# Attention in trips of 64 queries and four batches, with plain float32 scores, ahead of a recurrence

## The chip, the cores and the metric

The kernel runs on one core of one Trainium2 chip. Times are device microseconds of that core, from one launch. The core has five engines that run their own instruction streams: PE (TensorE, matrix products; PEld are its weight loads), DVE (VectorE), ACT (ScalarE), POOL (GpSimd) and SP (SyncE, which here only issues DMAs). They wait for one another by semaphores.

## The reference

Eight batches of 512 tokens with 512 features pass a causal attention layer with 16 heads of 32 features, and then a recurrence over the 512 tokens. Each result is added to its input. cond is one vector for each batch; it gives the attention one key and one value more ("image"), and the recurrence its first state.

```python
q_word, k_word, v_word = jnp.split(x @ c_attn_w + c_attn_b, 3, axis=-1)
k = jnp.concatenate([k_img, k_word], axis=1)       # k_img, v_img: from cond
v = jnp.concatenate([v_img, v_word], axis=1)
scores = jnp.einsum('bhqd,bhkd->bhqk', q, k) / jnp.sqrt(jnp.float32(HDIM))
scores = jnp.where(causal[None, None], scores, jnp.float32(MASK_OUT)) + mask
attn = jax.nn.softmax(scores, axis=-1)
out = jnp.einsum('bhqk,bhkd->bhqd', attn, v)
out = out.transpose(0, 2, 1, 3).reshape(B, S, EMBED)
x = x + (out @ c_proj_w + c_proj_b)

xw = jnp.einsum('ntd,dh->nth', x, Wx) + b
def step(prev_h, xw_t):
    next_h = jnp.tanh(prev_h @ Wh + xw_t)
    return (next_h, next_h)
x = x + hs                                           # hs: all 512 states, from h0 = cond
```

## The kernel before

**Tiling.** Attention runs in 16 trips. A trip takes 128 queries (one block of tokens) of two batches, blocks outermost, so that four trips finish a block for all eight batches. In a trip stand 32 units, one for each batch and head. Causality lets a unit of block p (0 to 3) look at 128 (p + 1) keys. A unit is a score product (`score`, L928), a subtraction with mask and row minimum on DVE (L791), the exponential with its sum on ACT (L648), transposes of 128 columns each (`turn`, L938) whose copies alternate between DVE (L800) and ACT (L655), and, for each group of four units, value products (`pv`, L951): for every key tile four products, one for each head, with 32 weight columns each, so in four column groups of the array.

**Precision.** Projections run as three products of float32r halves (`split_product`, L466 to L468). For the scores, q and k are split too: ACT writes the high halves (L641), DVE the low ones (L766), and six DMAs for each chunk of four heads store them in `kq_dram` (L478). Three DMAs bring a group's tile back (L540), with the three parts under one another in 96 partitions, and one float32r product of 96 rows makes a unit's scores. The scores of the image key are four short products for each chunk (L915, L917). Value products, recurrence and input products are plain float32 products.

**Recurrence.** A step (L1004) is 16 plain products with 32 weight columns, four for each of the four column groups of the array, from the states to `rec`; DVE transposes the result (L842), ACT takes the tanh (L694), and the next step needs that. Every four steps share input products (`xsteps`, L995, 16 products; `xpart` is a quarter of them). Tokens of block b can be stepped when block b is through attention, so its 128 steps are spread over the four trips of block b + 1 (STEPS = 32 a trip). The steps from FIRST = 384 on stand after the last trip, alone.

**Order.** `main_order` lays the events of a trip out by unit: transposes lag four units behind the scores, value products ten; at unit 10 the projection of the trip before begins (`proj`, L835 on DVE), behind it the load of x for the next but one trip (`xload`, L520), at unit SPLIT_AT the next trip's x is split (`xsplit`, L628 on ACT), and from unit 10 + FREE the next trip's q, k and v are made. `order` spreads the steps evenly over the estimated cost and turns this into one list for each engine; each engine works through its list in order. LAGS shifts an engine's list against PE's. SP issues the loads of key and value tiles as places come free: tile groups in a ring of ROOM columns (`tile_places`), values in VTILES buffers.

## Time and profile before

| | us |
|---|---|
| median of 3 runs | 1697.04 |
| lowest, highest | 1691.76, 1697.95 |
| the profiled execution | 1689.44 |
| its span, first to last instruction | 1687.6 |

The profile has one execution. Its rows give, for each instruction or group of instructions, the line of the kernel, the engine, what is written and read, and the count; PE's busy time includes the latency at the end of a product, so two blocks that follow one another closely overlap in it, and a block's own time is better read as the distance to the next start. A plain float32 product stands as two instructions in the records (the 16 products of a step are x32), a float32r product or a transpose as one. "Idle before" names what ended an engine's wait.

### The profile page before, as it was taken

The page shows a single profiled execution, that of the slowest core. Times are in us where ns is not written, and L with a number is a line of the kernel's source. Part 1 is how long each engine was busy: PE and PEld are TensorE (multiplying, and loading weights), DVE is VectorE, ACT ScalarE, POOL GpSimd, SP SyncE. Part 2 cuts the span into 40 slices and gives each one's busy share as a digit, 9 for nine tenths or more (in the row PEclk, how much of TensorE's full clock was granted, in tenths as well). Part 3 has the DMA queues.
Part 4 walks back from the last instruction along what each step waited for, and adds up shares of the span by engine and source line. Part 5 has one row for each costly group of instructions (what it writes and reads, how often), then busy time and mean ns, then how long its engine had stood idle before and what let it go on. Part 6 is the DMA issues. An engine that isn't in the chain of part 4 may idle for free.

```text
span 1687.6 us, 65682 instructions
## 1 busy us (share of the span) xinstructions
PE 1521.2 (90%) x28397; PEld 1288.2 (76%) x28397; DVE 817.9 (48%) x2592; ACT 718.4 (43%) x2289; POOL 369.9 (22%) x535
## 2 busy tenths in 40 slices
PE   6589988999999999999999988999999999777775
PEld 6478777778877878888888877888888788666664
DVE  4455554454545455555555545555565555222221
ACT  3355553444444444544445444454454545111111
POOL 2045552203131222203132130311313100000000
PEclk9799899999999999999999999999999999999999
DMA  7655555334344454445545445555555632000000
GB/s 252 184 186 179 166 181 145 111 96 124 106 126 116 120 145 132 129 110 144 143 137 151 112 136 148 142 156 133 151 140 156 165 89 70 9 15 10 15 9 15
DMA packets 139936, 204.73 MB, mean 121 GB/s; under 512 B 19432, under 2 KB 91240, under 8 KB 139136
## 3 DMA queue, kind: packets, MB, share of 16 engines
q1 hardware_dynamic: 112640, 128.05, 28.9%
q0 software_dynamic: 27008, 72.47, 13.0%
q8 instruction: 226, 3.70, 1.0%
q14 instruction: 62, 0.51, 0.1%
HBM read 133.06 MB, written 67.37 MB: 119 GB/s over the span
## 4 chain that ended last, share of the span: by engine, by line
PE 79%; DMA 6%; DVE 5%; issue 4%; ACT 4%; SPq 2%; POOL 0%; DVEq 0%; ACTq 0%; POOLq 0%
PE rec L1004 24%; PE turned L938 10%; PE dense L466 7%; PE dense L467 6%; PE dense L468 6%; PE rec L995 5%; PE scores L928 5%; PE pv L951 4%; PE scores L1004 4%; DMA xin<-x 3%; DVE pre L842 3%; ACT states L694 2%; PE pv L969 2%; DMA kq<-kq_dram 1%; PE dense L1011 1%
## 5 line engine op out<-in xcount | busy, mean ns | idle before, releaser
L1004 PE MATMUL rec<-wh,states 128*32 128x128 f32 x14336 | 485.2, 276 | 62.9 <-ACT states L694 61.3
L1004 PEld LDWEIGHTS rec<-wh,states 128*32 128x32 f32 x14336 | 376.0, 110 | 129.1 <-ACT states L694 90.7
L648 ACT ACTIVATE probs<-probs,nmax 128x128 f32<-128x128 f32 (+3 forms) x512 | 287.4, 562 | 209.5 <-DVE nmax L791 203.0
L694 ACT ACTIVATE states<-pre 128x32 f32<-128x32 f32 x512 | 133.3, 260 | 431.3 <-DVE pre L842 430.3
L842 DVE STREAM_TRANSPOSE pre<-rec 128x128 f32<-128x128 f32 x448 | 141.6, 316 | 342.1 <-PE rec L1004 338.9
L791 DVE CUSTOM_DVE_ANT_0 probs<-scores,msk,nimg 128x128 f32<-128x128 f32 (+3 forms) x512 | 276.2, 544 | 61.8 <-PE scores L928 54.5
L938 PE MATMUL turned<-ident,probs 128*128 128x128 f32 x1280 | 243.7, 290 | 13.1 <-ACT probsT L655 11.7
L928 PE MATMUL scores<-kq 96*128 96x128 f32 (+3 forms) x512 | 204.9, 403 | 18.5 <-DMA kq<-kq_dram 16.7
L938 PEld LDWEIGHTS turned<-ident,probs 128*128 128x128 f32 x1280 | 145.4, 141 | 78.8 <-issue 55.7
L800 DVE COPY probsT<-turned 128x128 f32<-128x128 f32 (+3 forms) x256 | 124.6, 487 | 80.1 <-PE turned L938 75.7
L655 ACT COPY probsT<-turned 128x128 f32<-128x128 f32 (+3 forms) x256 | 107.0, 418 | 95.8 <-PE turned L938 94.2
L995 PE MATMUL rec<-wx,x 128*32 128x128 f32 x3584 | 131.7, 278 | 10.9 <-ACT rec L620 10.7
L466 PE MATMUL dense<-xT_hi,wqkv_hi 128*128 128x256 f32 x464 | 139.8, 301 | 0.6 <-DVE ks_lo L766 0.6
L478 POOL DMA_DIRECT2D kq_dram<-qs_hi x120 | 86.3, 722 | 224.2 <-DVE qs_lo L766 215.1
L467 PE MATMUL dense<-xT_lo,wqkv_hi 128*128 128x256 f32 x464 | 135.1, 291 | 0.0
L468 PE MATMUL dense<-xT_hi,wqkv_lo 128*128 128x256 f32 x464 | 134.3, 290 | 0.0
L928 PEld LDWEIGHTS scores<-kq 96*128 96x128 f32 x512 | 103.0, 201 | 36.9 <-DMA kq<-kq_dram 17.9
L591 POOL DMA_DIRECT2D out<-outs x32 | 20.4, 639 | 490.4 <-ACT outs L684 490.4
L995 PEld LDWEIGHTS rec<-wx,x 128*32 128x32 f32 x3584 | 101.9, 134 | 27.2 <-issue 13.5
L478 POOL DMA_DIRECT2D kq_dram<-ks_hi x120 | 86.5, 721 | 87.9 <-DVE ks_lo L766 87.5
L951 PE MATMUL pv<-probsT,vbuf 128*32 128x128 f32 x2560 | 98.0, 281 | 7.8 <-DMA vbuf<-v_dram 7.8
L648 ACT ACTIVATION_READ_ACCUMULATOR probs<-probs,nmax 128x1 f32 x512 | 95.9, 187 | 0.0
(159 smaller groups left out, 2218.6 us busy)
## 6 DMA issues: line engine op xcount, KB each, us to landing
kq<-kq_dram SPq DMA_DIRECT2D x96, 320.0 KB, 5.2
kq<-kq_dram SPq DMA_DIRECT2D x96, 256.0 KB, 4.4
kq<-kq_dram SPq DMA_DIRECT2D x96, 192.0 KB, 3.6
kq_dram<-qs_hi POOLq DMA_DIRECT2D x120, 128.0 KB, 2.9
kq_dram<-ks_hi POOLq DMA_DIRECT2D x120, 128.0 KB, 3.4
kq<-kq_dram SPq DMA_DIRECT2D x96, 128.0 KB, 2.8
xin<-x SPq DMA_DIRECT2D x32, 256.0 KB, 4.0
v_dram<-vbuf POOLq DMA_DIRECT2D x32, 256.0 KB, 3.1
```

Source lines behind the costliest of these rows:

```text
L466: pe.matmul(out, hi, moving_hi, start=first, stop=False)
L467: pe.matmul(out, hi, moving_lo, start=False, stop=False)
L468: return pe.matmul(out, lo, moving_hi, start=False, stop=last)
L478: eng.dma_start(kq_dram[part, r, :, i, :, at:at + P], src[:, i % 2, :].bitcast(F32).rearrange("p (e t) -> p e t", e=2)).then_inc(stored[i ...
L648: act.activation(probs[:, g % PROBS, 0:n], probs[:, g % PROBS, 0:n], ACT.Exp, scale=-1.0, bias=nmax[:, e, h:h + 1], accum_out=rowsum[:, e, ...
L694: act.activation(state_cells(g), pre[:].rearrange("p f (b z) -> p f b z", z=GROUP)[:, :, :, s], ACT.Tanh).then_inc(h_ready, 1)
L791: dve.tensor_tensor_reduce(out=probs[:, g % PROBS, 0:n], in0=scores[g % 2][:, 0:n], in1=msk[:, e, 0:n], scale=-SCALE, scalar=nimg[:, trip ...
L842: dve.transpose(pre_all, rec_bank(g // GROUP)[:, 0:P]).then_inc(pre_ready, 1)
L928: pe.matmul(scores[g % 2][:, 0:n], heads_tile(group)[0:3 * Q, j, 0:P], heads_tile(group)[0:3 * Q, j, P:P + n], start=True, stop=True).then ...
L938: last = pe.transpose(turned[g % 2][:, P * k:P * k + P], probs[:, g % PROBS, P * k:P * k + P], ident[:])
L995: pe.matmul(rec_bank(g)[Q * j:Q * j + Q, 0:P], x1_group(g)[:, f], wx[:, f, :].rearrange("p (a j c) -> p a j c", a=C, j=C)[:, :, j, :], sta ...
L1004: last = pe.matmul(rec_bank(g // GROUP)[Q * j:Q * j + Q, 0:P], state_tile(g - 1)[:, f, :], wh[:, f, P * j:P * j + P], start=False, stop=f ...
```

## The change

A trip takes 64 queries of four batches. There are still 16 trips and 32 units in each; a unit is now one head of two batches, whose 64 queries each fill the 128 partitions. Blocks become parts of 64 tokens, so key lengths run from 64 to 512 in steps of 64, and the transposes and value products of an odd number of parts end with half a tile. The steps of a part are spread over the two trips of the next part, 32 in each, and FIRST is 448: 64 steps stand after the last trip.

q stays in SBUF in float32 (ACT adds the bias), k is written once by DVE, stored by one DMA for each chunk and loaded by one DMA for each group; the splits, `kq_dram` and their semaphores go. Scores are plain float32 products: for each unit two, one for each batch, with the 32 rows of the head (a row group of the array) and 64 weight columns (half of the column groups). Units are emitted in pairs, whose heads lie in neighbouring row groups. Image scores are four plain products for each chunk. Value products are for one batch and 64 queries, so twice as many with half the columns. x is loaded in four pieces for each trip, since a trip takes half of the tokens of two of the stored tiles. VTILES is 2, with two batches in each buffer; the ring of key tiles holds three of the longest.

```diff
-TRIPS = BLOCKS * PAIRS
+W = P // 2
+PARTS = S // W
+QUADS = 2
+PAIRED = 2
+TRIPS = PARTS * QUADS
...
-STEPS = S // (BLOCKS * PAIRS)
+STEPS = W // QUADS
...
-FIRST = (BLOCKS - 1) * P
-
-PROBS = 4
+FIRST = S - W
+
+PROBS = 5
...
-FREE = (7, 5, 5, 5, 5)
-SPLIT_AT = (15, 14, 14, 14, 14)
-VTILES = 3
+SPLIT_AT = (16, 16, 15, 15, 15, 15, 15, 15)
+CHUNK_AT = (18, 18, 16, 16, 16, 16, 16, 16)
+VTILES = 2
...
         if u < HEADS:
+            if u % 2 == 0:
+
+                emit([("score", v, 0, 0.07 + 0.107 * keys(g) / P) for v in (u, u + 1)])
             if u % HC == HC - 1:
                 loads += [("kqload", group, 0, 0.0) for group in range(GROUPS) if PLACES[group][0] == u // HC + 1]
-            emit([("score", u, 0, max(0.11, 0.053 * (block_of(g) + 1)) + 0.1)])
...
-        def store_parts(eng, kind, g, i):
...
+        def store_keys(eng, g, i, stored):
+            p, r = divmod(g, QUADS)
+            eng.dma_start(k_dram[4 * r:4 * r + 4, i, :, W * p:W * p + W].rearrange("b p t -> p b t"),
+                          knew[:, i, :].rearrange("p (b t) -> p b t", b=4)).then_inc(stored, 16)
...
+        def load_x(eng, g):
+
+            p, r = divmod(g, QUADS)
+            for k in range(2):
+                for pair in range(PAIRED):
+                    eng.dma_start(xin[:, g % 2, pair, 2 * k:2 * k + 2, :].rearrange("p f (e t) -> p (f e) t", e=2),
+                                  x[p // 2 * PAIRS + 2 * r + pair, :, 2 * k:2 * k + 2, :]
+                                  .rearrange("p f (e t) -> p (f e) t", e=2)[:, :, W * (p % 2):W * (p % 2) + W]
+                                  ).then_inc(x_loaded[g % 2][k], 16)
...
-                    for part in range(3):
-                        sp.dma_start(heads_tile(g)[Q * part:Q * part + Q].bitcast(F32),
-                                     kq_dram[part, r, :, c, e, 0:P + P * (p + 1)]
-                                     .rearrange("(j d) t -> d j t", d=Q)).then_inc(tile_loaded[g % LOADS], 16)
+                    sp.dma_start(heads_tile(g), k_dram[4 * r + 2 * e:4 * r + 2 * e + 2, c, :, 0:keys(trip)]
+                                 .rearrange("b p t -> p b t")).then_inc(tile_loaded[g % LOADS], 16)
...
+                    whole, left = divmod(keys(trip), P)
+                    for b in range(2):
+                        mine = v_dram[4 * r + 2 * e + b, 0:keys(trip), P * c:P * c + P]
+                        if whole:
+                            sp.dma_start(vtile[g % VTILES][:, b, 0:whole, :],
+                                         mine[0:P * whole].rearrange("(n q) d -> q n d", q=P)
+                                         ).then_inc(v_loaded[g % VTILES], 16)
+                        if left:
+                            sp.dma_start(vtile[g % VTILES][0:left, b, whole, :], mine[P * whole:P * whole + left]
+                                         ).then_inc(v_loaded[g % VTILES], 16)
...
-                elif kind in ("q", "k"):
+                elif kind == "q":
                     wait_dense(act, kind, g, i)
...
+                    act.activation(q[:, g % 2, i, :], bank(kind, g, i)[:, 0:2 * P], ACT.Identity,
+                                   bias=bqk[:, 0, i:i + 1]).then_inc(copied(kind, g, i), 1)
...
+                elif kind == "k":
+                    wait_dense(dve, kind, g, i)
+                    if g:
+                        wait_stored(dve, g - 1, i)
+                    dve.tensor_scalar(knew[:, i, :], bank(kind, g, i)[:, 0:2 * P], bqk[:, 1, i:i + 1], None,
+                                      ALU.add).then_inc(copied(kind, g, i), 1)
...
+                        for b in range(2):
+
+                            n = 2 * e + b
+                            last = pe.matmul(d[W * b:W * b + W, HC * e:HC * e + HC], q[:, g % 2, i, W * n:W * n + W],
+                                             kimg[:, i, 4 * r + n, :], start=True, stop=True, skip_group_check=True)
...
-                    pe.matmul(scores[g % 2][:, 0:n], heads_tile(group)[0:3 * Q, j, 0:P],
-                              heads_tile(group)[0:3 * Q, j, P:P + n], start=True, stop=True).then_inc(scores_ready, 1)
+
+                    rows = slice(Q * j, Q * j + Q)
+                    for b in range(2):
+                        at = W * (2 * e + b)
+                        last = pe.matmul(scores[g % 2][W * b:W * b + W, 0:n], q[rows, trip % 2, c, at:at + W],
+                                         heads_tile(group)[rows, b, :], start=True, stop=True, skip_group_check=True)
+                    last.then_inc(scores_ready, 1)
...
+                    for at in range(0, n, P):
+                        last = pe.transpose(turned[g % 2][0:min(P, n - at), at:at + P],
+                                            probs[:, g % PROBS, at:min(at + P, n)], ident[:])
...
+                    for at in range(0, n, P):
+                        rows = slice(0, min(P, n - at))
+                        for b in range(2):
+                            mine = slice(at + W * b, at + W * b + W)
+                            for j in range(HC):
+
+                                last = pe.matmul(pv[Q * j:Q * j + Q, P * c + W * b:P * c + W * b + W],
+                                                 vtile[g % VTILES][rows, b, at // P, Q * j:Q * j + Q],
+                                                 probsT[rows, (HC * g + j) % TURNED, mine],
+                                                 start=c == 0 and b == 0 and at == 0, stop=False, skip_group_check=True)
```

PE's stream, in a trip with 384 keys before (between a step and the next projection products). Transposes write turned, scores go to scores0 and scores1, L1004 is the step.

```order
L1004 MATMUL rec<-wh,states 32x128 x16
L938 MATMUL turned1<-ident,probs 128x128 x3
L928 MATMUL scores1<-kq 128x384
L951 MATMUL pv<-probsT,vbuf 32x128 x12
L1004 MATMUL rec<-wh,states 32x128 x16
L1011 MATMUL dense0<-ident,hist 128x128 x4
L938 MATMUL turned0<-ident,probs 128x128 x3
L928 MATMUL scores0<-kq 128x384
...
L938 MATMUL turned1<-ident,probs 128x128 x3
L928 MATMUL scores1<-kq 128x384
L938 MATMUL turned0<-ident,probs 128x128 x3
L928 MATMUL scores0<-kq 128x384
```

The same place in a trip with 320 keys of the change; L963 are the scores, L974 the transposes, L991 the value products, L1035 and L1044 input products and step.

```order
L1044 MATMUL rec<-wh,states 32x128 x16
L991 MATMUL pv<-probsT,vbuf 32x64 x24
L974 MATMUL turned0<-ident,probs 128x128 x2
L974 MATMUL turned0<-ident,probs 64x128
L963 MATMUL scores0<-kt,q 64x320 x2
L1035 MATMUL rec<-wx,x1 32x128 x16
L1044 MATMUL rec<-wh,states 32x128 x16
L963 MATMUL scores1<-kt,q 64x320 x2
...
L963 MATMUL scores0<-kt,q 64x320 x2
L1044 MATMUL rec<-wh,states 32x128 x16
L1051 MATMUL dense0<-ident,hist 128x128 x4
L963 MATMUL scores1<-kt,q 64x320 x2
```

One 96x128-weight score for each unit has become two of 32x64, shown as x2; a pair stands together or has a step or other products between its units.

SP's list at the start, before: six stores and three loads stand ahead of the first scores.

```order
L511 DMA x1<-w_proj 128x512 [waits low_ready]
L511 DMA x1<-w_proj 128x512 x3
L478 DMA kq_dram<-qs_hi 128x2x128 [waits dense_copied0]
L478 DMA kq_dram<-qs_hi 128x2x128
L478 DMA kq_dram<-qs_lo 128x2x128
L478 DMA kq_dram<-ks_hi 128x2x128 [waits dense_copied1]
L478 DMA kq_dram<-ks_lo 128x2x128
L478 DMA kq_dram<-ks_hi 128x2x128
L540 DMA kq<-kq_dram 32x4x256 [waits k_stored_first0,q_stored_first0]
L540 DMA kq<-kq_dram 32x4x256 x2
```

SP's list at the start, with the change:

```order
L542 DMA x1<-w_proj 128x512 x4
L498 DMA k_dram<-knew 128x4x64 [waits dense_copied1]
L568 DMA kt<-k_dram 128x2x64 [waits k_stored_first0] x2
L498 DMA k_dram<-knew 128x4x64 [waits dense_copied1]
L568 DMA kt<-k_dram 128x2x64 [waits k_stored_first1]
L498 DMA k_dram<-knew 128x4x64 [waits dense_copied1]
L568 DMA kt<-k_dram 128x2x64 [waits k_stored_first2]
```

Ahead of the first tile stands one store, and a load is one DMA.

ACT's list ahead of the split of the next trip's x (`xT_hi`), before, in a trip with 256 keys:

```order
L694 ACTIVATE states<-pre 128x32 [waits hist_kept,pre_ready]
L648 ACTIVATE probs,rowsum<-probs,nmax 128x256 [waits shifted_ready]
L694 ACTIVATE states<-pre 128x32 [waits pre_ready]
L648 ACTIVATE probs,rowsum<-probs,nmax 128x256 [waits shifted_ready]
L694 ACTIVATE states<-pre 128x32 [waits pre_ready]
L684 COPY outs<-dense1 128x4x4x32 [waits out_stored,dense_ready]
L620 COPY rec<-kimg 128x128 [waits pre_ready]
L694 ACTIVATE states<-pre 128x32
L655 COPY probsT<-turned1 128x256 [waits pv_done,turned_ready]
L628 CAST xT_hi<-xin 128x512 [waits dense_ready,x_loaded0_0]
L628 CAST xT_hi<-xin 128x512 [waits dense_ready,x_loaded0_1]
```

ACT's list at the same place with the change, in a trip with 192 keys:

```order
L724 ACTIVATE states<-pre 128x32 [waits hist_kept,pre_ready]
L724 ACTIVATE states<-pre 128x32 [waits pre_ready]
L676 ACTIVATE probs,rowsum<-probs,nmax 128x192 [waits shifted_ready] x2
L724 ACTIVATE states<-pre 128x32 [waits pre_ready]
L714 COPY outs<-dense1 128x4x4x32 [waits out_stored,dense_ready]
L659 COPY rec<-bxrows 128x128 [waits pre_ready]
L724 ACTIVATE states<-pre 128x32
L683 COPY probsT<-turned1 128x256 [waits pv_done,turned_ready]
L724 ACTIVATE states<-pre 128x32 [waits hist_kept,pre_ready]
L666 CAST xT_hi<-xin 128x512 [waits dense_ready,x_loaded0_0]
L666 CAST xT_hi<-xin 128x512 [waits dense_ready,x_loaded0_1]
```

The split (two instructions, the last rows) stands one unit later in the change, behind one step more; the probabilities of the next units are queued behind it in both.

## Rows read from the trace of the kernel before

**Rows 1.** The page's first part: busy time and share of the span.
```profile
PE 1521.2 (90%) x28397; PEld 1288.2 (76%) x28397; DVE 817.9 (48%) x2592; ACT 718.4 (43%) x2289; POOL 369.9 (22%) x535
```
**Rows 2.** Stretches: us, busy PE, PEld, DVE, ACT, POOL, PEclk, DMA share, GB/s.
```profile
75.00:267.00 192.00, 175.63 (x1379) 149.79 (x1378) 107.63 (x480) 103.73 (x402) 86.74 (x128) 0.92 0.56 174
267.00:1460.00 1193.00, 1141.81 (x21966) 966.73 (x21966) 630.51 (x1880) 549.84 (x1673) 266.73 (x376) 0.99 0.46 126
1460.00:1687.00 227.00, 159.32 (x4800) 132.51 (x4800) 50.32 (x151) 40.88 (x158) 4.78 (x8) 0.99 0.05 12
```
**Rows 3.** Chain of waits in a bare step: start us, us, what; last row: PE's timeline.
```profile
1500.15 1.13 PE rec L1004 x32
...
1501.30 0.33 DVE pre L842
...
1501.65 0.27 ACT states L694
...
1501.96 1.12 PE rec L1004 x32
...
1501.05 0.40 PE L995 MATMUL scores<-wx,x 128*32 128x128 f32 x8
```
**Rows 4.** PE's timeline (start us, busy us, line, tiles, count), untiled float32 products.
```profile
29.68 3.68 PE L906 MATMUL turned<-wh,spread 128*128 128x512 f32 x8
```
**Rows 5.** PE's timeline in the window of 1500.14 to 1500.18 us.
```profile
1500.15 0.32 PE L1004 MATMUL rec<-wh,states 128*32 128x128 f32 x4 [0.51 <-ACT states L694]
```
**Rows 6.** PE's timeline across changes of tiling, from 901 us.
```profile
901.32 0.49 PE L938 MATMUL turned<-ident,probs 128*128 128x128 f32 x3
901.73 1.08 PE L1004 MATMUL rec<-wh,states 128*32 128x128 f32 x32
902.75 0.44 PE L928 MATMUL scores<-kq 96*128 96x384 f32 x1
...
903.91 0.55 PE L938 MATMUL turned<-ident,probs 128*128 128x128 f32 x3
```
**Rows 7.** PE's timeline: input products and the step behind them.
```profile
910.17 1.14 PE L995 MATMUL rec<-wx,x 128*32 128x128 f32 x32
911.12 1.06 PE L1004 MATMUL rec<-wh,states 128*32 128x128 f32 x32
```
**Rows 8.** PE's timeline around scores of 384 and of 128 columns.
```profile
1005.81 0.55 PE L938 MATMUL turned<-ident,probs 128*128 128x128 f32 x3
...
1006.37 0.17 PE L915 MATMUL dense<-kimgx,qs_hi 128*128 128x8 f32 x1
...
1006.74 0.55 PE L938 MATMUL turned<-ident,probs 128*128 128x128 f32 x3
...
91.56 0.33 PE L938 MATMUL turned<-ident,probs 128*128 128x128 f32 x1
...
91.79 0.33 PE L466 MATMUL rec<-xT_hi,wqkv_hi 128*128 128x256 f32 x1
```
**Rows 9.** PE's timeline around a score of 512 columns (it lies between).
```profile
1290.33 0.66 PE L938 MATMUL turned<-ident,probs 128*128 128x128 f32 x4
...
1291.14 1.08 PE L1004 MATMUL rec<-wh,states 128*32 128x128 f32 x32
```
**Rows 10.** Groups by line and form: value products, all of them.
```profile
L951 PE MATMUL pv<-probsT,vbuf 128*32 128x128 f32 x2560 | 98.0, 281 | 7.8 <-DMA vbuf<-v_dram 7.8
```
**Rows 11.** Waits of ACT: us in total, times, longest.
```profile
ACT xT_hi L628 <- DMA xin<-x: 37.3, 18, 3.3
```
**Rows 12.** Timeline of SP and of PE around the second split of x.
```profile
120.64 0.83 SPq L520 DMA_DIRECT2D xin<-x  x2
...
125.63 0.30 PE L938 MATMUL turned<-ident,probs 128*128 128x128 f32 x1 [3.88 <-ACT probsT L655]
```
**Rows 13.** PE's timeline: the first scores and the first value products.
```profile
47.88 0.47 PE L928 MATMUL scores<-kq 96*128 96x128 f32 x1 [8.01 <-DMA kq<-kq_dram]
...
71.62 0.66 PE L951 MATMUL pv<-probsT,vbuf 128*32 128x128 f32 x8 [7.76 <-DMA vbuf<-v_dram]
```

More of the change, by code:

```diff
@@ L75, in tile_places @@
     for group in range(GROUPS):
[L76 removed]
+        size = 2 * keys(group // 8)
         if at + size > ROOM:
@@ L86, with v_loads @@
 PLACES = tile_places()
+def v_loads():
+    counts = []
+    for group in range(GROUPS):
+        n = keys(group // 8)
+        mine = 2 * (n // P > 0) + 2 * (n % P > 0)
+        counts.append(mine + (counts[group - VTILES] if group >= VTILES else 0))
+    return counts
+V_LOADS = v_loads()
 def main_order():
@@ L176, in order @@
     place = {}
-    for b in range(BLOCKS - 1):
-        first = ends[(b + 1) * PAIRS - 1] + 1
-        for n in range(PAIRS):
-            last = begins[(b + 1) * PAIRS + n]
+    for b in range(PARTS - 1):
+        first = ends[(b + 1) * QUADS - 1] + 1
+        for n in range(QUADS):
+            last = begins[(b + 1) * QUADS + n]
             whole = sum(w for *_, w in main[first:last])
@@ L198, in put @@
         for name, lags in LAGS.items():
-            if kind in ("q", "k") and name == ("POOL" if g == 0 else "SP"):
+            if kind == "k" and name == ("POOL" if g == 0 else "SP"):
                 continue
@@ L318, in attention_recurrence @@
         vnew = vbuf[:, 0:2 * D].rearrange("p (e d) -> p e d", e=2)
-        vtile = [vbuf[:, 2 * D + n * BLOCKS * P:2 * D + (n + 1) * BLOCKS * P].rearrange("p (n d) -> p n d", d=P)
-                 for n in range(VTILES)]
+        vtile = [vbuf[:, 2 * D + 2 * n * BLOCKS * P:2 * D + 2 * (n + 1) * BLOCKS * P]
+                 .rearrange("p (b n d) -> p b n d", b=2, d=P) for n in range(VTILES)]
         rinvx = spread[:, 0, :].rearrange("p (h q) -> p h q", h=H)
@@ L501, in _ @@
                 if n == C:
-                    for k in range(2):
-                        sp.dma_start(xin[:, 0, 2 * k:2 * k + 2, :], x[0, :, 2 * k:2 * k + 2, :]
-                                     ).then_inc(x_loaded[0][k], 16)
+                    load_x(sp, 0)
                 f, half = divmod(i, 2)
@@ L936, in _ @@
                         pe.wait_ge(turned_copied[g % 2], g // 2)
[L937 to L938 removed]
+                    for at in range(0, n, P):
+                        last = pe.transpose(turned[g % 2][0:min(P, n - at), at:at + P],
+                                            probs[:, g % PROBS, at:min(at + P, n)], ident[:])
                     last.then_inc(turned_ready, 1)
                 elif kind == "pv":
[L941 removed]
+                    n = keys(g // 8)
                     c = g % C
```

299 lines of the change are left out of this document (129 added, 170 removed).

## The prediction

> **What bounds the kernel now.** I read the page's busy shares first [rows 1]: TensorE is busy for 90% of the span, VectorE for 48%, ScalarE for 43%. Cut into stretches [rows 2], the span has three regimes. Up to 75 us the kernel starts up. From 75 to 267 us run the trips without recurrence steps, with TensorE busy for 176 of 192 us. From 267 to 1460 us attention and 384 recurrence steps share TensorE, which is busy for 1142 of 1193 us. The last 227 us are 128 steps with nothing beside them, and there one step follows the other through three engines: the chain [rows 3] shows 1.13 us of products, 0.33 of VectorE's transpose, 0.27 of ScalarE's tanh, and the next step starts 1.81 us after the one before. So a step costs 1.81 us when it stands alone, and only its time on TensorE when it is hidden. Up to 1460 us the question is how much TensorE has to do; the other engines wait for it. Busy counts the latency at the end of each block, so I price TensorE's work by distances between starts.
>
> **Two facts about TensorE that carry the sum.** First, the price of a plain float32 product. It is recorded as two instructions (16 products of a step are x32). Eight such records, 512 columns wide and untiled, take 3.68 us [rows 4], so about 0.43 us each, 0.84 ns a column. A step's 32 records of 128 columns take 0.90 us until the next block starts [rows 3]; alone at 0.84 ns a column they would take 3.4. Thus four column groups run at once and a record costs 0.027 us. A window of 0.04 us at a step's start holds the starts of four records [rows 5].
> Second, changing the tiling costs time. Transposes take some 0.109 us each (four are busy 0.66, three 0.55 [rows 6, 9]), yet the step behind three of them starts 0.41 us after the first, 0.08 more than 0.33 [rows 6]. The 32 records of that step hand over to an untiled score after 1.02 us, where a handover within the tiling took 0.90 [rows 3, 6], so 0.12 more. Three transposes behind another tiling are busy 0.55 us, behind the same one 0.49 [rows 6], 0.06 more; and a step behind another tiling 1.08 against 1.06 [rows 6, 7]. In and out is 0.28 us, 0.14 for each change. This speaks against the change. The Trainium skill says the same ("TensorEngine Tiling (Array Packing)", Key Properties: changing the tiling mode drains TensorE) without a price; by the rows the trace agrees.
>
> **The change part by part,** against the profiled span of 1687.6 us (its run took 1689.4; the median of the runs shown is 1697.0).
> (a) 64 of the 128 exposed steps go: 64 x 1.81 = -116. They come back in the hidden part at 0.90 each, +58, with their 16 groups of input products, which were spread over idle time and now stand as blocks of 32 records: 0.95 us from such a block to the step [rows 7], 16 x 0.90 = +14 with the first load taken with the changes.
> (b) Tiling changes. In the built programs the rows x columns of neighbouring TensorE instructions change 887 times before and 1539 times after: every pair of scores is an island of 32x64 among transposes and steps, image scores become 128x64, and odd parts end a value product with 64 rows. 652 x 0.14 = +91. Nothing hides it. The tilings 32x64 and 64x32 stand nowhere in the trace; for a change to them I take the price of 128x32, and for its bounds 0.08 and 0.20 (the dearest in-step above together): +52 to +130.
> (c) Scores go away: a 384-column score between transposes and the next untiled block adds 0.23 us (0.56 less 0.33), a 128-column one 0.12 [rows 8], a 512-column one 0.28 (0.81 less 0.44 and the 0.09 of a change) [rows 9]; with 0.18 in between for 256, 128 x (0.12 + 0.18 + 0.23 + 0.28) = -104.
> (d) New scores: per unit two products (two batches, 64 columns of the array each), so four records of n columns at 0.84 ns. n is 64 to 512 and 288 in the mean, against 320 before. How many of the four tiles (two row groups, two column groups) run at once is the open point: no instruction of the trace uses row groups beside each other. From below, all eight records of a pair at once as fast as one, 0.84 n a pair: 61 us in all. From above, column halves together but row groups in turn: 512 x 1.67 x 288 = 246. I take what independent tiles give, as column groups do in [rows 3]: a pair costs two records' depth, 1.67 n, and a unit that stands alone the same. The new order has 199 pairs back to back and 114 units alone (a step or a block of x products between them): 313 x 1.67 x 300 = +157.
> (e) Image scores: four products limited by weight loads, 0.37 us [rows 8], 64 times, about -26; eight short records with half as many weight columns, two tiles at once, about +14. Net -12.
> (f) Value products double in number with 64 instead of 128 columns: 2560 records x 0.109/4 = 70 us before [rows 10], 5120 records after. If a record keeps to its columns, 0; if four cannot start faster than in 0.109 us, +70. Four started within 0.04 us [rows 5], so I take 0. The number of transposes stays 1280, as half tiles still stream 128 columns of the identity.
> The TensorE page of the Trainium skill ("TensorE: Matmul & The Clock Gate", Wait — 56ns, not 53.3ns?) has a floor of about 25 ns between starts, by which the value products would not gain from fewer columns. Four starts within 40 ns [rows 5] speak against it; a burst is no stream.
> (g) DVE and ScalarE: the q and k splits go (two of VectorE's operations for each column chunk, and one of ScalarE's two), key lengths fall by a tenth, the x1 writes come in four pieces instead of two, and VectorE stays near half busy. They lie beside TensorE: 0. What they can change is waits.
> (h) Waits. TensorE was idle for 98 of the first 1460 us (75 to 1460: 67.6 us by [rows 2]; the rest in the start). ScalarE waits 37.3 us for x in 18 places, as its queue is in order and probabilities stand behind [rows 11]; TensorE follows with gaps such as 3.88 us at 125.6 [rows 12]. x is asked for at 120.64, when the projection of two trips ago is copied, and split two units later. The split now comes one to two units later, so with 3 us a unit most of this is gone although the x load is in four DMAs of 256-byte pieces. About -34. The first scores waited 8.01 us for their tile behind six stores and three loads, the first values 7.76 us [rows 13]; now one store and one load go before it: about -12. SP queues behind its waits for value products, as before.
> Sum: -116 + 58 + 14 + 91 - 104 + 157 - 12 + 0 - 55 = **+33 us**: 1721 for the span, and 1697 + 33 = 1730 beside the median.
>
> **The rivals.**
> R1, row groups or halves overlap more than I take. Four records of one unit started together in [rows 5]; if these belong to two tiles only, a unit needs 0.84 n and standing alone costs nothing: 512 x 0.84 x 288 = 123, 34 less, 1696, no change. For: the burst. Against: a record would then run at twice the untiled rate. R1b, the other side: eight records of a pair at once, 61 us, 96 less, 1634. It decides from about 113 us for all scores.
> R2, row groups take turns: 246, +89, 1819. For: nothing in the trace shows them together. The Trainium skill ("TensorE: Matmul & The Clock Gate", Measured speedup vs the span model) has 3.07x for four row groups, against R2; no row here shows it.
> R3, the value products don't get shorter, (f): +67 to +70, 1800. That is what the floor above would give; the sum of it is made of [rows 5, 7].
> R4, the waits stay: the x load with its small pieces and the shared dense banks keep ScalarE waiting, +55, 1785. Or they vanish: -43, 1687.
> That the change doesn't do what it says: the 64 steps can't all fit. Seven parts of 64 steps in 14 trips of over 80 us is 32 x 1.81 = 58 us of chain a trip; they fit.
>
> **How the numbers follow.** Forecast 0.38, R1 0.22, R1b 0.11, R2 0.13, R3 0.07, R4 0.06 and 0.03. The error of (b) and (h) is about 30 us on each. Measurement of this kernel can tell about 0.5% (8.5 us) from no change. Faster by over 0.5%: R1b, a third of R1, a seventh of the forecast and half of what is left, 0.29. Within: 0.14. Slower: 0.57. The range leaves out half of R1b and half of R2 and the ends: 1645 to 1815. The likeliest case alone has 1700 to 1762.
>
> **What would show it.** The last stretch of bare steps should be 64 x 1.81 = 116 us. The scores' blocks in the timeline: start to next start near 1.67 n ns for a pair (0.8 us at n = 512 plus 0.14) and as much for a lone unit; half of it is R1, double R2. A value block of one key tile and eight products should last 0.22 us to the next start; 0.44 is R3. ScalarE's wait for x should be under 10 us and the first score start before 45 us; else R4. I am wrong as a whole if a change of tiling around the scores costs far less than 0.14.

## The result, and the profile after

The changed kernel takes 1743.5 us (median of 4 runs, 1733.6 to 1749.6), the kernel before 1695.6 beside it: a ratio of 1.028, 95% interval 1.023 to 1.033. It is slower, by 48 us, where I had forecast 33. The profiled execution has a span of 1741.3 us, 53.7 more than before, and it is the one to take apart. First its page, part 1 (as [rows 1]), then the start and the three stretches of [rows 2], cut where the steps begin and where the last work beside them ends (us, busy PE, PEld, DVE, ACT, POOL, PEclk, DMA share, GB/s).

```profile
PE 1654.6 (95%) x32749; PEld 1263.7 (73%) x32749; DVE 798.4 (46%) x2687; ACT 670.5 (39%) x2257; POOL 184.6 (11%) x300
```
```profile
0.00:50.00 50.00, 35.70 (x249) 31.28 (x250) 19.14 (x49) 15.85 (x32) 11.47 (x26) 0.86 0.65 217
50.00:177.00 127.00, 115.89 (x1182) 90.73 (x1180) 57.68 (x282) 51.06 (x223) 19.18 (x34) 0.77 0.25 65
177.00:1613.00 1436.00, 1416.86 (x28741) 1073.56 (x28739) 694.18 (x2273) 581.73 (x1921) 150.99 (x235) 1.00 0.28 76
1613.00:1741.00 128.00, 86.14 (x2581) 68.15 (x2580) 27.37 (x84) 21.86 (x83) 2.98 (x5) 0.96 0.05 13
```

Start and step-free trips together shrink from 267 to 177 us, the tail of bare steps from 227 to 128, but the shared stretch grows from 1193 to 1436: it now carries 448 steps and 14 trips. TensorE is busy there for 98.7% of the time, so nothing but its own work counts. The table sums that work over all records, each from its start to the next record's start, with the waits between taken out (us). The waits are listed below it; "all else" is smaller work and the few us ahead of the first record and behind the last.

| on TensorE | before | after |
|---|---|---|
| scores | 138 | 210 |
| transposes of probabilities | 138 | 191 |
| image scores | 29 | 22 |
| value products | 87 | 95 |
| split products (q, k, v, projection) | 401 | 419 |
| steps | 501 | 504 |
| input products of the steps | 138 | 125 |
| waits in the last stretch | 59 | 32 |
| other waits | 92 | 38 |
| all else | 105 | 106 |

Scores and transposes took 125 us more; the waits gave back 80. Two places of the timeline show the new blocks (start, us busy, line, tiles, count): a pair of scores at n = 448, then a lone unit at the same n (n is the number of keys, so of columns); the pair at 1192.17 and the lone unit at 1198.05 repeat them.

```profile
1178.06 0.98 PE L963 MATMUL scores<-kt,q 32*64 32x448 f32 x8
1178.97 1.08 PE L1044 MATMUL rec<-wh,states 128*32 128x128 f32 x32
1179.98 1.09 PE L974 MATMUL turned<-ident,probs 128*128 128x128 f32 x8
...
1208.36 0.97 PE L963 MATMUL scores<-kt,q 32*64 32x448 f32 x4
1209.25 1.08 PE L1044 MATMUL rec<-wh,states 128*32 128x128 f32 x32
1210.27 0.97 PE L963 MATMUL scores<-kt,q 32*64 32x448 f32 x4
1211.16 0.39 PE L492 MATMUL dense<-xT_hi,wqkv_hi 128*128 128x256 f32 x1
```

Eight records take 0.91 us to the next start, four take 0.89. Over the medians of all blocks at each n from 128 to 512, a pair costs 1.667 n + 164 ns and a lone unit 1.667 n + 151 ns: the second unit of a pair costs 14 ns. The step between goes on to the next tiling after 1.01 us, where [rows 3] has 0.90 within one.

### The profile page after: what moved, and what is told of

The parts are those of the page before. It is cut to its first block, busy times and chain, and to the rows that moved or that the text cites. A ratio compares the mean times of both kernels' runs of the same rounds, so it can differ in the third digit from the quotient of the medians.

```text
span 1741.3 us, 74131 instructions
## 1 busy us (share of the span) xinstructions
PE 1654.6 (95%) x32749; PEld 1263.7 (73%) x32749; DVE 798.4 (46%) x2687; ACT 670.5 (39%) x2257; POOL 184.6 (11%) x300
## 4 chain that ended last, share of the span: by engine, by line
PE 89%; issue 3%; DVE 2%; DMA 2%; ACT 2%; SPq 1%; POOL 0%; DVEq 0%; ACTq 0%; POOLq 0%
PE rec L1044 26%; PE scores L963 11%; PE turned L974 11%; PE dense L492 8%; PE dense L493 7%; PE dense L494 7%; PE rec L1035 6%; PE pv L991 5%; PE pv L1009 2%; PE scores L1044 2%; DVE pre L870 1%; ACT states L724 1%; PE dense L945 1%; PE dense L1051 1%; SPq L517 1%
## 5 line engine op out<-in xcount | busy, mean ns | idle before, releaser
L1044 PE MATMUL rec<-wh,states 128*32 128x128 f32 x15360 | 516.4, 275 | 27.0 <-ACT states L724 25.8
L1044 PEld LDWEIGHTS rec<-wh,states 128*32 128x32 f32 x15360 | 399.7, 110 | 123.3 <-ACT states L724 64.3
L676 ACT ACTIVATE probs<-probs,nmax 128x64 f32<-128x64 f32 (+7 forms) x512 | 271.6, 531 | 269.7 <-DVE nmax L815 266.6
L815 DVE CUSTOM_DVE_ANT_0 probs<-scores,msk,nimg 128x64 f32<-128x64 f32 (+7 forms) x512 | 249.9, 514 | 62.8 <-PE scores L963 54.4
L974 PE MATMUL turned<-ident,probs 128*128 128x128 f32 (+1 forms) x1280 | 242.9, 292 | 7.9 <-ACT probsT L683 7.2
L963 PE MATMUL scores<-kt,q 32*64 32x64 f32 (+7 forms) x2048 | 231.4, 431 | 0.3 <-DVE nmax L815 0.2
L974 PEld LDWEIGHTS turned<-ident,probs 128*128 128x128 f32 (+1 forms) x1280 | 132.5, 135 | 90.4 <-issue 66.3
L1035 PE MATMUL rec<-wx,x 128*32 128x128 f32 x3840 | 133.7, 275 | 4.3 <-ACT rec L659 4.0
L1035 PEld LDWEIGHTS rec<-wx,x 128*32 128x32 f32 x3840 | 99.0, 109 | 29.5 <-ACT rec L659 12.0
L492 PEld LDWEIGHTS dense<-xT_hi,wqkv_hi 128*128 128x128 f32 x488 | 94.2, 193 | 24.1 <-issue 23.0
L991 PE MATMUL pv<-probsT,vbuf 128*32 128x64 f32 (+1 forms) x5120 | 104.9, 223 | 4.5 <-DMA vbuf<-v_dram 4.5
L963 PEld LDWEIGHTS scores<-kt,q 32*64 32x64 f32 x2048 | 65.2, 133 | 57.8 <-issue 48.0
L991 PEld LDWEIGHTS pv<-probsT,vbuf 128*32 128x32 f32 (+1 forms) x5120 | 84.8, 110 | 22.5 <-issue 16.0
L498 POOL DMA_DIRECT2D k_dram<-knew x60 | 47.0, 783 | 504.7 <-DVE knew L791 483.7
```

The lines of the kernel that those rows point to most:

```text
L492: pe.matmul(out, hi, moving_hi, start=first, stop=False)
L676: act.activation(probs[:, g % PROBS, 0:n], probs[:, g % PROBS, 0:n], ACT.Exp, scale=-1.0, bias=nmax[:, e, h:h + 1], accum_out=rowsum[:, e, ...
L815: dve.tensor_tensor_reduce(out=probs[:, g % PROBS, 0:n], in0=scores[g % 2][:, 0:n], in1=msk[:, e, 0:n], scale=-SCALE, scalar=nimg[:, trip ...
L963: last = pe.matmul(scores[g % 2][W * b:W * b + W, 0:n], q[rows, trip % 2, c, at:at + W], heads_tile(group)[rows, b, :], start=True, stop=T ...
L974: last = pe.transpose(turned[g % 2][0:min(P, n - at), at:at + P], probs[:, g % PROBS, at:min(at + P, n)], ident[:])
L991: last = pe.matmul(pv[Q * j:Q * j + Q, P * c + W * b:P * c + W * b + W], vtile[g % VTILES][rows, b, at // P, Q * j:Q * j + Q], probsT[rows ...
```

## The experiments

All ratios are to the kernel before, run on the same chip; "the changed kernel" stands at 1743 us, 1.028.

**1. Are row groups beside each other what makes a pair fast?** Both units of a pair read the same 32 rows.

```diff
-                    rows = slice(Q * j, Q * j + Q)
+                    rows = slice(Q * (j // 2 * 2), Q * (j // 2 * 2) + Q)
```

> Only the rows of the array that the second unit of each pair uses are changed: it reads the same 32 rows of q and keys as the first (so the scores of half the heads are those of the neighbouring head, and the output is another one). The order and the 1539 tiling changes are those of the changed kernel. Theory (the pair is fast since its units sit in different row groups): the pair costs 3.33 n + 0.16 us in place of 1.67 n + 0.16, 199 x 1.67 ns x 300 = +100 us, about 1843. Rival, the overlap has nothing to do with row groups (records of one unit leave gaps that any record can fill): 1743, no change.

Measured: 1815 us, ratio 1.073 (1.069 to 1.077), so +72 beside the median of the changed kernel. The timeline has pairs at n = 384:

```profile
1103.24 1.51 PE L963 MATMUL scores<-kt,q 32*64 32x384 f32 x8
1104.68 0.39 PE L492 MATMUL dense<-attnT_hi,wproj_hi 128*128 128x256 f32 x1
...
1113.85 1.51 PE L963 MATMUL scores<-kt,q 32*64 32x384 f32 x8
1115.29 0.87 PE L974 MATMUL turned<-ident,probs 128*128 128x128 f32 x6
```

A pair takes 1.44 us, which is 3.33 n + 0.16; by the formula above it takes 0.80 in different rows. Two row groups do run at once, and R2 (row groups in turn) falls by a direct test. My +100 for the sum took 300 columns for the mean of the pairs; it is 269, which gives +89, and TensorE's time in scores did grow by 87 us (210 to 297). That the kernel lost only 72 is mostly the clock: the split products took 8 us less, at a granted clock of 0.89 between 50 and 177 us instead of 0.77.

**2. Units one by one, and pairs never parted.** First every unit alone, as the scores were issued before the change; then no step between the two units of a pair.

```diff
-            if u % 2 == 0:
-                emit([("score", v, 0, 0.07 + 0.107 * keys(g) / P) for v in (u, u + 1)])
+            emit([("score", u, 0, 0.07 + 0.107 * keys(g) / P)])
```

> The scores are issued unit by unit, as before the change, never as a pair: 512 lone units in place of 199 pairs and 114 lone ones; tiling changes rise from 1539 to 1894. Theory (row groups run beside each other, a lone unit leaves half of them empty): 199 more runs of 1.67 ns x 288 = +96 us, 355 changes x 0.13 = +46, together +142: about 1885 us. Rival, row groups take turns anyway: only the changes, +46, 1790. Rival, a change of tiling costs nothing on its own: +96, 1840. The start of a lone unit to the next start should stay at 1.67 n + 151 ns.

```diff
                 done += main[at][3]
+                if main[at][0] == "score" and main[at][1] % 2 == 0 and at + 1 < last:
+                    continue
```

> No recurrence step is put between the two units of a pair of scores any more: 256 pairs and no lone unit, where the changed kernel has 199 pairs and 114 lone units; the tiling changes on TensorE fall from 1539 to 1480. Theory (four tiles, two row groups by two column halves, run at once, and a change of tiling costs 0.12 to 0.14 us): 57 runs of scores fewer at 1.67 ns x 300 columns = -28 us, and 59 x 0.13 = -8, so about 1707 us where the changed kernel takes 1743. Rival, row groups bring nothing (a pair lasts as long as two lone units): only the -8, 1735. Rival, the steps that now come in twos behind a pair wait for their chain of 0.9 us: up to 57 x 0.5 = 28 us come back, and TensorE's idle time grows from 70 us to near 100.

Measured: 1879 us (ratio 1.109, 1.106 to 1.113), +135 where the theory had +142; and 1704 us (1.007, 1.005 to 1.009), -40 by the medians and -36 by the ratios, where it had -36. TensorE's waits did not grow (74 us after 70), so the rival with steps that wait falls. So 36 to 40 of the 48 us that the change lost are the 57 pairs that its own step placement cut in two. Between these two kernels lie 256 runs of scores, 256 x 1.67 x 288 ns = 123 us, and 414 tiling changes; the 52 us left are 0.126 for a change, if a block more costs nothing else.

**3. What does a change of tiling cost by itself?** Small products of 4 columns were put ahead of the transposes of every unit, once on 32 rows and 32 columns, once untiled.

```diff
+                    pe.matmul(turned[g % 2][0:Q, 0:4], ident[0:Q, 0:Q], ident[0:Q, 0:4], start=True, stop=True, skip_group_check=True)
```
```diff
+                    pe.matmul(turned[g % 2][0:P, 0:4], ident[:], ident[:, 0:4], start=True, stop=True, skip_group_check=True)
```

> Ahead of the transposes of every unit, in the bank that they overwrite, stands one more product of 4 columns on 32 rows and 32 columns of the array: 512 products, and the tiling changes rise from 1539 to 2161. Its twin (the next kernel) has the same products untiled and no more changes. Theory (0.14 us for a change): 622 x 0.14 = 87 us more than its twin; by the order kernel, whose TensorE work fell 31 us for 372 changes, 0.084 each: +52. Rival, changes only cost where a long product drains: under +20 over its twin.

> The twin: the 512 products of 4 columns untiled, in the same places, 1539 tiling changes as in the changed kernel. Theory: a short untiled product costs some 0.05 us beside transposes, 512 x 0.05 = +26 us, about 1769 (from 1758 to 1785).

Measured: 1827 us (1.081, 1.077 to 1.085) with the islands, 1854 (1.096, 1.093 to 1.100) without them: the one with fewer changes is slower. Both theories missed, because the two are no twins. The timeline of the untiled one:

```profile
1200.35 0.39 PE L973 MATMUL turned<-ident 128*128 128x4 f32 x2
1200.59 0.53 PE L975 MATMUL turned<-ident,probs 128*128 128x128 f32 x3
...
1204.95 0.28 PE L973 MATMUL turned<-ident 128*128 128x4 f32 x2
1205.10 0.53 PE L975 MATMUL turned<-ident,probs 128*128 128x128 f32 x3
```

Four columns untiled cost 0.15 us among untiled blocks and 0.24 behind a step: 111 us for 512, 0.22 each, against my 0.05. The price of a short product is not in its columns. So I made a pair with equal products: 432 of them in the tiling of the steps, once ahead of transposes (1823 changes), once ahead of hidden steps (1539).

```diff
+                    if g >= HEADS - 432:
+                        pe.matmul(turned[g % 2][0:Q, 0:4], ident[:, 0:Q], ident[:, 0:4], start=True, stop=True, skip_group_check=True)
```
```diff
+                    if g < 432:
+                        pe.matmul(rec[0:Q, 256:260], ident[:, 0:Q], ident[:, 0:4], start=True, stop=True, skip_group_check=True)
```

> Ahead of the transposes of 432 units stands one product of 4 columns in the tiling of the steps (128 rows by 32 columns of the array). Where the block ahead has another tiling, it is an island: 1823 tiling changes in place of 1539. Its twin (the next kernel) has the same 432 products ahead of hidden steps, whose tiling they share, and 1539 changes. The difference between the two is 284 changes and nothing else. At 0.14 us each 40 us, at 0.084 (what the order kernel saved on TensorE for 372 changes) 24, at 0.12 34. Rival, a change costs only where a long product has to drain, not beside a short one: under 10 us.

> The twin: 432 products of 4 columns directly ahead of hidden steps, in their tiling, 1539 changes as in the changed kernel. Two records at the 0.027 us of a step's record are 0.06 us: 432 x 0.06 = +24 us if nothing else moves, 1767; if a record behind another of the same column tile has to wait for its end (0.11 us), +50 to +80.

The second opens an accumulation anew in the bank in which the steps accumulate, so its recurrent states are other ones; its instructions are the same. Measured: 1785 us (1.054, 1.051 to 1.057) and 1764 us (1.042, 1.039 to 1.045). The difference of 20.8 us over 284 changes is 0.073 us each (0.05 to 0.10 by the scatter of the runs); by the sums of TensorE's work (1717 and 1689 us) it is 0.097. So a change is not free, as the rival had it. But these are no exact twins either. Ahead of a step the trace shows of the small product

```profile
1154.79 0.19 PE L1043 MATMUL rec<-ident 128*32 128x4 f32 x1
1154.80 0.31 PE L1046 MATMUL rec<-wh,states 128*32 128x128 f32 x3
```

that three records of the step start between its two; it cost 0.043 us (18.5 us of work for 432). Ahead of transposes, behind a block of its own tiling (the first three lines) and between two blocks of transposes (the others), the timeline is this:

```profile
1154.54 1.06 PE L1046 MATMUL rec<-wh,states 128*32 128x128 f32 x32
1155.41 0.20 PE L974 MATMUL turned<-ident 128*32 128x4 f32 x2
1155.55 0.55 PE L976 MATMUL turned<-ident,probs 128*128 128x128 f32 x3
...
1170.68 0.55 PE L976 MATMUL turned<-ident,probs 128*128 128x128 f32 x3
1171.16 0.23 PE L974 MATMUL turned<-ident 128*32 128x4 f32 x2
1171.31 0.66 PE L976 MATMUL turned<-ident,probs 128*128 128x128 f32 x4
```

In the first case the step and the product take 1.01 us together, as a step alone does in the changed kernel. Over all places between 180 and 1600 us at which TensorE did not wait, the medians against the same places of the changed kernel are: +0.018 us where the product adds no change (behind steps and whole value products), +0.155 where it adds one (behind scores, image scores and half value products), +0.25 where it adds two (between untiled blocks). That is 0.137 for one change and 0.115 each for the two. With the product at 0.018 instead of 0.043, the twins would give 0.11 by the times and 0.13 by the work. So my 0.14 was somewhat high, not double.

**4. Exposed steps.** 64 steps go back into the tail, all else stays.

```diff
-FIRST = S - W
+FIRST = S - 2 * W
-    for b in range(PARTS - 1):
+    for b in range(PARTS - 2):
```

> The steps of the last two parts stand exposed at the end, 128 as before the change, the rest is the changed kernel's. Theory: 64 x 1.81 = +116 us, their 64 hidden steps go at 0.90 each, -58, and 16 groups of input products at 0.90, -14, which then stand in the idle time of the bare steps; 69 tiling changes fewer at 0.12, -8, and 11 runs of scores fewer, -6: together +30, about 1773 us where the changed kernel takes 1743. Last stretch 128 x 1.81 = 232 us. Rival, a hidden step costs more than its 0.90 (waits for its chain or drives the trips apart): then less than +15, under 1758. Rival, it costs nothing since it fills idle time of TensorE: +116, 1859.

Measured: 1767 us (1.044, 1.041 to 1.047), +24 by the medians and +28 by the ratios. Hiding the 64 steps is worth 24 to 28 us here, close to the +30 expected. So the change's other parts cost some 74.

**5. An order that follows the tiling.** If changes cost, an order with fewer should beat both kernels. Transposes come in twos, projections stand beside them, and a small dynamic programme places the steps.

```diff
+        if u % 2 == 0 and TURN_LAG <= u < HEADS + TURN_LAG:
+            emit([("turn", v, 0, 0.05 + 0.11 * tiles_of(v // UNITS)) for v in (u - TURN_LAG, u - TURN_LAG + 1)])
...
+        spots.append((at, done[-1], (before[at] != "column") + (after[at] != "column") - (before[at] != after[at])))
...
+                c = table[-1][p][0] + GAP_COST * max(0.0, GAP - work) ** 2
```

> The same work in an order that follows the tiling: the transposes of two units are issued together ahead of a pair of scores, what has no place of its own (projections, image scores) stands beside them, and a step goes where the tiling changes anyway or beside value products, spaced by a small dynamic programme; never within a pair. 256 pairs, no lone units, 1108 tiling changes in place of 1539. Theory (a change costs 0.12 to 0.14 us and nothing hides it): -28 for the lone units and 431 x 0.13 = -56, together -84: about 1659 us, faster than the kernel before (1696). Rival, changes of tiling are free or hidden: 1715. Rival, steps less evenly spread wait for their chain: each 0.2 us of wait on 448 steps gives back 90 us, and then TensorE's idle time of 70 us doubles.

Measured: 1714 us (1.013, 1.010 to 1.015), not 1659. Beside the kernel with pairs TensorE's work fell by 31 us. The expectation has 1108 changes; the program that ran has 1165, by the count that gives 1539 and 1480 for the kernels before it. So 31 us are for 315 changes, 0.099 each. But its waits rose from 74 to 117 us: the third case of the expectation, in small.

> The order that follows the tiling again, with steps kept at least 1.0 us of other work apart where this costs one tiling change (the first such kernel let TensorE wait 42 us more than the kernel with pairs only), image scores directly ahead of a pair of scores, transposes of the outputs beside other transposes, and x split one unit earlier: 1196 tiling changes, 256 pairs. Theory (a change costs 0.084 us as in the first such kernel, the waits go back to some 80 us): 1704 - 284 x 0.084 = 1680, with 5 to 10 us of waits 1685 to 1690, the time of the kernel before. Rival, waits stay at 110 us: 1710.

Measured: 1717 us (1.015, 1.013 to 1.018), the rival. The work stayed at 1597 us and the waits at 117, but they had moved. PE's timeline, and ACT's wait for x there, then in the changed kernel ([rows 11] for before), then in the next experiment:

```profile
1160.18 1.82 PE L1104 MATMUL rec<-wh,states 128*32 128x128 f32 x32 [3.86 <-ACT states L784]
```
```profile
ACT xT_hi L726 <- DMA xin<-x: 41.2, 24, 5.6
```
```profile
ACT xT_hi L666 <- DMA xin<-x: 16.8, 18, 3.6
```
```profile
ACT xT_hi L726 <- DMA xin<-x: 6.1, 5, 2.1
```

My own edit had caused it: I had moved the split of x a unit earlier, to where x had not landed, and tanh stands behind it in ScalarE's queue.

```diff
-SPLIT_AT = (15, 15, 14, 14, 14, 14, 14, 14)
-CHUNK_AT = (18, 18, 16, 16, 16, 16, 16, 16)
+SPLIT_AT = (16, 16, 16, 16, 16, 16, 16, 16)
+CHUNK_AT = (18, 18, 18, 18, 18, 18, 18, 18)
```

> The second order kernel with one thing moved: x is split for the next trip at unit 16 and its first products start at unit 18, where e_order2 had 14 and 16. In e_order2 ScalarE's in-order queue stood at the split until x had landed, and once a trip a recurrence step waited 2 to 4 us behind it (12 gaps of 2.0 to 4.1 us, about 40 us in all). Theory: these gaps go, TensorE's idle time falls from 117 to about 80 us, the time from 1717 to about 1680, faster than the kernel before by 10 us. Rival, the first products of a trip now come too late for its first scores: gaps at the start of each trip instead, 1700 to 1720.

Measured: 1687 us, ratio 0.998 (0.996 to 1.000), the time of the kernel before; waits 98 us. Of the 31 us won, 20 are waits; TensorE's work fell too, at a mean granted clock of 0.987 after 0.979. What was left showed on ScalarE and TensorE around one step:

```profile
1036.40 0.61 ACT L736 ACTIVATE probs<-probs,nmax 128x384 f32<-128x384 f32 x1 [0.86 <-DVE nmax L875]
1036.93 0.18 ACT L736 ACTIVATION_READ_ACCUMULATOR probs<-probs,nmax 128x1 f32 x1
1037.02 0.60 ACT L736 ACTIVATE probs<-probs,nmax 128x384 f32<-128x384 f32 x1
1037.52 0.19 ACT L736 ACTIVATION_READ_ACCUMULATOR probs<-probs,nmax 128x1 f32 x1
1037.62 0.43 ACT L751 ACTIVATE pimg<-dimg 64x16 f32<-64x16 f32 x2
1038.08 0.26 ACT L784 ACTIVATE states<-pre 128x32 f32<-128x32 f32 x1
...
1038.39 1.08 PE L1104 MATMUL rec<-wh,states 128*32 128x128 f32 x32 [1.40 <-ACT states L784]
```

The tanh at 1038.08 stands behind both exponentials of a pair, so the last edit moves only queues beside TensorE: the second exponential of a pair later, and the two halves of the x split a unit apart. TensorE's products are the same ones in the same order.

```diff
-            emit(begin(g + 1))
+            emit(begin(g + 1)[:1])
+        if g + 1 < TRIPS and h == SPLIT_AT[block_of(g)] + 1:
+            emit(begin(g + 1)[1:])
...
+                late = 0.9 if (name, kind) == ("ACT", "score") and g % 2 and 4 * UNITS <= g < HEADS - UNITS else 0.0
+                plan[name].append((clock + lags.get(kind, 0.0) + late, kind, g, i))
```

> TensorE's order is that of e_order3, only the orders of the engines beside it move: ScalarE takes the second exponential of a pair about 0.9 us later, so that the tanh of a step stands between the two (in e_order3 both, with the copy of x between them, stood ahead of it: 0.62 + 0.19 + 0.60 + 0.19 us, and TensorE waited 1.40 us at 1038.39), and the two halves of the x split are taken a unit apart. Theory (what separates e_order3, 1687, from the sum of its work on TensorE is 44 us of waits for steps between 177 and 1560 us, where the kernel with pairs only has 19): a third to half of it goes, 1665 to 1675, faster than the kernel before by 1%. Rival, VectorE's transpose is the late link (it stands behind two score passes of 0.6 us) and nothing is gained: 1687. Rival, later probabilities make the transposes wait: over 1690.

Measured: 1671 us (1668 to 1677), ratio 0.989, interval 0.985 to 0.992. It is faster than both kernels, by 1.1% and by 4%, with all parts of the change in it. Which of the two moves did how much was not taken apart, and whether an order of this kind would also help the kernel before was not run; so the 1.1% belongs to the change and the order together. TensorE's work is 1587 us and its waits 82; steps waited 23.4 us for tanh outside the tail, after 35.0:

```profile
PE rec L1107 <- ACT states L787: 23.4, 43, 0.9
```
```profile
PE rec L1104 <- ACT states L784: 35.0, 61, 2.6
```

## Why the prediction was right, and where its terms were not

Forecast 1730, measured 1743.5, slower as the likeliest case had it. On spans, +33 was forecast and +54 came. Step by step:

**(a) The tail.** Right. The last stretch is 128 us; from its first step's start to its last step's end it is 115 us, forecast 116, and the steps start 1.81 us apart:

```profile
1616.77 1.08 PE L1044 MATMUL scores<-wh,states 128*32 128x128 f32 x32 [0.50 <-ACT states L724]
1617.66 0.40 PE L1035 MATMUL rec<-wx,x 128*32 128x128 f32 x8
1618.58 1.08 PE L1044 MATMUL scores<-wh,states 128*32 128x128 f32 x32 [0.51 <-ACT states L724]
```

Steps, input products and the tail's waits fell by 37 us (698 to 661), forecast -44; experiment 4 has 24 to 28 with the changes of tiling and lone units that hiding brings.

**(b) to (e) Scores and tiling.** Together forecast +132 (91 - 104 + 157 - 12); scores, transposes and image scores went from 305 to 423 us, +118. The term that was the open point, (d), is right to the digit: 1.67 n for a pair and as much for a lone unit. Its fixed part is 0.15 us a run; 313 x 0.157 = 49 leaves 161 of the 210 us for the columns, against 157. R1, R1b and R2 fall by the timeline, R2 by experiment 1 as well: two row groups take 1.44 us in turn and 0.80 beside each other. The Trainium skill ("TensorE: Matmul & The Clock Gate", Measured speedup vs the span model) has 3.07x for four row groups; for two, these float32 products show 1.8x.
**(b)**, 0.14 us for a change, was high. The order kernel has 0.099, splitting pairs 0.126, small products put in place 0.115 to 0.137; the twins' 0.073 and 0.097 are too low, as experiment 3 shows. I had read in and out off one busy step, 0.28 us, and halved it. Of the 0.28, 0.20 are distances between starts and 0.08 are differences of busy time, which counts the end latency of blocks; the starts alone give 0.10 each. At 0.12, an estimate between these, the 652 changes are 78 us instead of 91, and the other terms of scores and transposes come to 40, where I had 41. My sign of being wrong as a whole, a price far below 0.14, did not show.
The count of changes needs a word. The 887 and 1539 take every transpose as untiled. In the built programs transposes of part of a tile have a smaller tiling, 128x64 for a half one, and with them counted there are 931 and 1821 changes. Those to half transposes cost nothing: behind a step and ahead of scores, two whole transposes and a half one (n = 320) take 0.48 us, as three whole ones (n = 384) do, at 16 and 13 such places. So the count that I took is the one to price.

```profile
898.23 0.55 PE L974 MATMUL turned<-ident,probs 128*128 128x128 f32 x3
898.71 0.77 PE L963 MATMUL scores<-kt,q 32*64 32x320 f32 x8
...
930.90 0.55 PE L974 MATMUL turned<-ident,probs 128*128 128x128 f32 x3
931.38 0.87 PE L963 MATMUL scores<-kt,q 32*64 32x384 f32 x8
```

That changes cost at all, as the Trainium skill says ("TensorEngine Tiling (Array Packing)", Key Properties), every one of these measurements shows.

**(f) Value products.** Taken as 0, measured +8 us; R3 (+67 to +70) falls. The 5120 records take 95 us, 18.5 ns each, where the 2560 wider ones took 87 us, 34 ns each. Counted by records, the floor of about 25 ns between starts in the Trainium skill ("TensorE: Matmul & The Clock Gate", Wait — 56ns, not 53.3ns?) would give 128 us, an estimate, and the trace disagrees. But a product of the program leaves two records; counted by products, 2560 at 37 ns each, the floor is not touched, so this trace refutes only my reading of it by records. A window on 16 records, eight products:

```profile
239.22 0.43 PE L991 MATMUL pv<-probsT,vbuf 128*32 128x64 f32 x16
239.47 1.06 PE L1035 MATMUL rec<-wx,x 128*32 128x128 f32 x32
```

0.25 us, forecast 0.22, where R3 had 0.44.

**(h) Waits and the clock.** Without the clock I had -46; outside the tail the waits fell from 92 to 38 us, -54. The first scores start at 40.88 us (47.88 before, [rows 13]), under the 45 that I asked for. ScalarE's wait for x fell from 37.3 [rows 11] to 16.8 us, not under 10. The clock is the step that failed in sign. I had -9 for fewer gaps, but the granted clock between 50 and 177 us is 0.77 where the step-free trips had 0.92 [rows 2]. The split products there take 0.185 us each (63 us for 341 records) and 0.151 in the next stretch, 11 us more; all split products together rose by 18 us, with 2688 records in both kernels. Why the clock was low is open. It fell to the lower of its two levels (1.2 GHz) behind gaps such as the first line's, but also from 93 to 110 us (the second line: us, busy PE to POOL, granted clock 0.51) and from 151 to 168, where TensorE was busy for 98% and had no gap of 1 us before; and e_order3 has gaps of 3.3 and 5.4 us in these trips and 0.88. So fewer gaps do not by themselves give the clock back, as my -9 took for granted.

```profile
57.78 0.65 PE L991 MATMUL pv<-probsT,vbuf 64*32 64x64 f32 x16 [4.50 <-DMA vbuf<-v_dram]
```
```profile
93.00:110.00 17.00, 16.78 (x106) 12.79 (x107) 5.84 (x30) 5.17 (x24) 1.83 (x4) 0.51 0.23 52
```

The balance against the forecast: tail +7, scores and tiling -14, value products +8, waits -8, split products with the clock +27, all else +1, together the 21 us between +33 and +54. That terms missed by +43 and -22 partly cancel is luck.

## What to carry to other kernels

Before tiling a product, count how often TensorE will change its tiling in the built order, price that at 0.10 to 0.14 us each, and let the order follow: here the same change loses 48 us in the order it came with and wins 19, with ScalarE's queue re-timed as well, in one that keeps pairs whole and groups blocks of one tiling. Products in different row groups share time only if nothing is placed between them, so a scheduler that drops other work by even spacing must know which neighbours belong together. And each time TensorE gets leaner, look at the in-order queues beside it again: twice a step waited behind a copy or an exponential that was merely earlier in ScalarE's list.

## What the runs showed of the hardware

- Two units of float32 scores in two row groups and two column halves take 14 ns more than one unit; in the same rows they take 1.8 times as long (1.44 against 0.80 us at n = 384).
- A 4-column float32 product costs 0.22 us untiled, 0.16 on 32x32 with the changes it brings (84 us of work for 512), 0.043 on 128x32 ahead of a step of that tiling, whose records start between its own two, and 0.018 on 128x32 behind one. I had expected 0.05 for the untiled one.
- The transposes (1280 in every kernel) take 138 us in long untiled stretches, 191 as islands between scores and steps, and 158 when grouped by two. The last one of a block holds TensorE for 0.20 us ahead of a tiled block, where one ahead of another transpose holds it for 0.11 (medians).
- A change of tiling costs 0.137 us where one is added and 0.115 each where two are (medians in e_small_turn); one to a half transpose costs nothing.
